# Loading, turning and splitting the left halves of x's first four tiles ahead of the right halves in a two-layer transformer kernel

## The reference

```
q = split_heads(hidden_states @ Wq)      # hidden_states: (2, 1024, 512), Wq: (512, 2048)
k = split_heads(hidden_states @ Wk)
v = split_heads(hidden_states @ Wv)
scores = einsum('bhsd,bhtd->bhst', q, k) * scaling + mask
attn = softmax(scores); out = einsum('bhst,bhtd->bhsd', attn, v)
x = layernorm(x + out @ Wo)
# ... then rows chosen by a router, attention and MLP over them, and a second layernorm
```

## Time and profile before

| | |
|---|---|
| time, median of three executions | 1269.94 us (1269.14 to 1270.07) |
| the profiled execution: time | 1268.86 us |
| the profiled execution: span of the trace | 1267.1 us |
| PE busy | 1252.8 us, 99% |
| DVE busy | 807.0 us, 64% |
| ACT busy | 623.2 us, 49% |
| POOL busy | 245.1 us, 19% |

### The profile page before, as it was taken

One profiled execution on the slowest core, in us unless ns is written; L12 is line 12 of the kernel. 1 busy time (PEld: TensorE's weight loads), 2 busy tenths in 40 slices (PEclk: granted clock), 3 DMA queues, 4 the chain that ended last, 5 costly groups with the idle time before them and its releaser, 6 DMA issues.

```text
span 1267.1 us, 19392 instructions
## 1 busy us (share of the span) xinstructions
PE 1252.8 (99%) x7474; PEld 1103.3 (87%) x7474; DVE 807.0 (64%) x2227; ACT 623.2 (49%) x1448; POOL 245.1 (19%) x216
## 2 busy tenths in 40 slices
PE   9999999999999999999999999999999999999997
PEld 8898989898989898988989898989898987568896
DVE  5555665656555655667776776565656579969633
ACT  5544444444544454555554444445444444558653
POOL 2101111020202020024220211111111113310155
PEclk9999999999999999999999999999999999999999
DMA  6000101010101110203320110110010106565563
GB/s 207 28 25 25 43 17 51 17 51 17 50 18 50 34 51 1 84 18 117 109 96 30 34 34 30 60 34 34 18 51 17 51 18 235 167 216 168 182 217 117
DMA packets 62445, 89.36 MB, mean 71 GB/s; under 512 B 3264, under 2 KB 36032, under 8 KB 62352
## 3 DMA queue, kind: packets, MB, share of 16 engines
q1 hardware_dynamic: 61936, 86.82, 20.8%
q0 software_dynamic: 416, 1.31, 0.3%
HBM read 79.20 MB, written 8.91 MB: 70 GB/s over the span
## 4 chain that ended last, share of the span: by engine, by line
PE 94%; DVE 3%; DMA 1%; ACT 1%; POOL 1%; issue 0%; POOLq 0%
PE proj L1170 45%; PE y L1170 14%; PE s L1170 12%; PE o L1170 10%; PE tp L1263 6%; PE proj L1178 2%; DVE arena L1696 1%; PE s L1178 1%; ACT arena L1480 1%; PE o L1178 1%; DMA late<-rope,position 0%; DMA wraw<-in_L_ffn_wq 0%; PE tp L1399 0%; PE y L1377 0%; DMA yacc<-in_L_attn_hidden_states 0%
## 5 line engine op out<-in xcount | busy, mean ns | idle before, releaser
L1170 PE MATMUL proj<-arena 128*128 128x256 f32 (+1 forms) x3504 | 647.3, 333 | 0.1
L1170 PEld LDWEIGHTS proj<-arena 128*128 128x128 f32 x3504 | 535.5, 189 | 60.2 <-DVE arena L1696 1.1
L2045 POOL TENSOR_TENSOR arena<-wraw,arena 128x1024 fp32r<-128x1024 f32 x73 | 174.8, 2402 | 826.8 <-ACT arena L1480 826.7
L1518 ACT ACTIVATE prob<-prob,stat 128x384 f32<-128x384 f32 (+1 forms) x256 | 150.8, 589 | 363.5 <-DVE stat L1731 363.0
L1696 DVE TENSOR_TENSOR arena<-proj,arena 128x512 fp32r<-128x512 f32 (+1 forms) x256 | 142.2, 557 | 239.7 <-ACT arena L1480 237.0
L1170 PE MATMUL y<-arena 128*128 128x512 f32 x816 | 211.6, 394 | 0.0
L1170 PE MATMUL s<-arena 128*128 128x384 f32 (+2 forms) x912 | 203.6, 338 | 0.7 <-DVE arena L1696 0.6
L1696 DVE TENSOR_TENSOR arena<-tp,arena 128x384 fp32r<-128x384 f32 (+2 forms) x258 | 134.8, 522 | 93.2 <-ACT arena L1480 92.4
L1170 PE MATMUL o<-arena 128*128 128x256 f32 (+2 forms) x966 | 191.9, 319 | 0.0
L1480 ACT ACTIVATE arena<-proj 128x512 fp32r<-128x512 f32 (+1 forms) x256 | 124.3, 486 | 130.7 <-PE proj L1170 114.0
L1170 PEld LDWEIGHTS s<-arena 128*128 128x128 f32 x912 | 157.6, 188 | 17.2 <-DVE arena L1696 1.8
(11 more groups left out here) (163 smaller groups left out, 669.4 us busy)
## 6 DMA issues: line engine op xcount, KB each, us to landing
wraw<-in_L_attn_Wv SPq DMA_DIRECT2D x16, 512.0 KB, 3.4
wraw<-in_L_attn_Wo SPq DMA_DIRECT2D x16, 512.0 KB, 3.7
wraw<-in_L_attn_Wq SPq DMA_DIRECT2D x15, 512.0 KB, 3.4
wraw<-in_L_attn_Wk SPq DMA_DIRECT2D x15, 512.0 KB, 3.4
yacc<-in_L_attn_hidden_states SPq DMA_DIRECT2D x16, 256.0 KB, 3.6
y_dram<-yacc SPq DMA_DIRECT2D x16, 256.0 KB, 2.2
out<-works SPq DMA_DIRECT2D x16, 256.0 KB, 2.7
wraw<-in_L_ffn_wq SPq DMA_DIRECT2D x8, 512.0 KB, 4.6
```

The lines of the kernel that those rows point to most:

```text
L1170: ins = e.matmul(out_ap, l[a], r[b], start=first and i == 0 and j == 0, stop=final and i == n - 1 and j == 2, skip_group_check=skip)
L1518: e.activation(prob[s][:, 0:n], prob[s][:, 0:n], ACT.Exp, bias=stat[:, 4 * s + 1:4 * s + 2], scale=-1.0, accum_out=stat[:, 4 * s + 2:4 * s ...
L2045: e.tensor_tensor(lo, wraw[n % RAW_SLOTS][:], hi.bitcast(F32), ALU.subtract).then_inc(*G_.inc("wsplit", n, "lo"))
```

## The change

The loads, turns and splits of x's tiles 0 to 3 in the first batch are each done in two halves of 256 columns. A new job `residleft` loads the left half of a tile and a new job `turnleft` turns it (two transposes) and makes its high and low part; the old jobs `resid` and `turn` do the right half for these tiles. The right halves are loaded between the two halves of weight piece 0. In the sequence of jobs, `turnleft` stands where `turn` stood; then comes the split of the first half of piece 0 and `qkfirst`; then the four right `turn` jobs, the split of the second half of piece 0, and `qk`; the splits of piece 1 come behind that.

```
+HALVED = 4
...
                     for half in range(2):
                         first_loaded[2 * n + half].plan(n)
                         job("wloadhalf", n, half)
+                        if (n, half) == (0, 0):
+                            for t in range(HALVED):
+                                load_resid(0, t)
...
-        for t in range(4):
-            load_resid(0, t)
+        for t in range(HALVED):
+            left_loaded[t].plan()
+            job("residleft", t)
         load_next(2)
...
         for t, to in enumerate(("tp", "s0", "s1", "o0")):
-            turn_x(0, t, to)
+            hold(to, ("turnleft", t), V_, "turn", 0, t, "lo")
+            job("turnleft", t)
+            bank_of["turn", 0, t] = to
             if t % 2 == 1:
                 job("warm", 1 + t // 2)
-        need("q", 0, 0)
+        job("wfirst", 0, 0)
+        bank_of["qk", 0, "q", 0] = "proj0"
+        hold("proj0", ("qk", 0, "q", 0), V_, "qk", 0, "q", 0, "lo")
+        job("qkfirst", 0, "q", 0)
+        for t in range(HALVED):
+            job("turn", 0, t)
+        job("wfirst", 0, 1)
+        split_on[0], split_to[0] = "V", 1
+        load_next()
+        job("qk", 0, "q", 0)
         need("k", 0, 0)
-        put(project_qk(0, "q", 0))
...
+                elif kind == "turnleft":
+                    t, = key
+                    dst = bank[bank_of["turn", 0, t]]
+                    pe.wait_ge(*freed(bank_of["turn", 0, t], "turnleft", t))
+                    pe.wait_ge(*left_loaded[t].at())
+                    for k in range(KT // 2):
+                        ins = e.transpose(dst[:, k * P:(k + 1) * P], yacc[:, t, k * P:(k + 1) * P], ident[:])
+                    ins.then_inc(*T_.inc("turnleft", t, "made"))
...
-                        pe.wait_ge(*V_.at("turn", b, c * 4 + 3, "lo"))
+                        pe.wait_ge(*(V_.at("turnleft", HALVED - 1, "lo") if (b, c) == (0, 0) else V_.at("turn", b, c * 4 + 3, "lo")))
...
                     else:
                         pe.wait_ge(*split(which, b, h // HG))
+                        pe.wait_ge(*V_.at("turn", b, c * 4 + 3, "lo"))
                         ins = three_passes(e, bank[to][:, :], pairs[KT // 2:], False, True)
```

More of the change, by code:

```diff
@@ L434, in build @@
         resid_loaded = [Landings(semaphore(f"resid_loaded{t}")) for t in range(TT)]
+        left_loaded = [Landings(semaphore(f"left_loaded{t}")) for t in range(HALVED)]
         y_stored = [Landings(semaphore(f"y_stored{t}")) for t in range(TT)]
@@ L448, in build @@
             const=dict(V=("ones", "zeros", "masks", "small"), G=("ident0", "ident", "filled", "small")),
+            turnleft=dict(T=("made",), S=("hi",), V=("lo",)),
             turn=dict(T=("made",), S=("hi",), V=("lo",)),
@@ L1196, in tensor_program @@
                     dst = bank[bank_of["turn", b, t]]
-                    pe.wait_ge(*freed(bank_of["turn", b, t], "turn", b, t))
+                    halved = b == 0 and t < HALVED
+                    if not halved:
+                        pe.wait_ge(*freed(bank_of["turn", b, t], "turn", b, t))
                     if b == 0:
@@ L1204, in tensor_program @@
                         pe.wait_ge(*x_loaded[t % 6].at(b, t))
-                    for k in range(KT):
+                    for k in range(KT // 2 if halved else 0, KT):
                         ins = e.transpose(dst[:, k * P:(k + 1) * P], src[:, k * P:(k + 1) * P], ident[:])
@@ L1492, in scalar_program @@
                         act.wait_ge(*T_.at("qk", NH - 1, "k" if t < 4 else "q", t // 4, "made"))
+                    ks = slice(KT // 2 if b == 0 and t < HALVED else 0, KT)
                     src = bank[bank_of["turn", b, t]][:, :].rearrange("p (k n) -> p k n", k=KT)
                     act.wait_ge(*T_.at("turn", b, t, "made"))
-                    hi_part(xT[0][:, :, t * P:(t + 1) * P], src, "turn", b, t)
+                    hi_part(xT[0][:, ks, t * P:(t + 1) * P], src[:, ks, :], "turn", b, t)
+                elif kind == "turnleft":
+                    t, = key
+                    src = bank[bank_of["turn", 0, t]][:, 0:D // 2].rearrange("p (k n) -> p k n", k=KT // 2)
+                    act.wait_ge(*T_.at("turnleft", t, "made"))
+                    hi_part(xT[0][:, 0:KT // 2, t * P:(t + 1) * P], src, "turnleft", t)
                 elif kind == "qk":
@@ L1709, in vector_program @@
                     cols = slice(t * P, (t + 1) * P)
+                    ks = slice(KT // 2 if b == 0 and t < HALVED else 0, KT)
                     src = bank[bank_of["turn", b, t]][:, :].rearrange("p (k n) -> p k n", k=KT)
-                    lo_part(xT[1][:, :, cols], src, xT[0][:, :, cols], "turn", b, t)
+                    lo_part(xT[1][:, ks, cols], src[:, ks, :], xT[0][:, ks, cols], "turn", b, t)
+                elif kind == "turnleft":
+                    t, = key
+                    cols = slice(t * P, (t + 1) * P)
+                    src = bank[bank_of["turn", 0, t]][:, 0:D // 2].rearrange("p (k n) -> p k n", k=KT // 2)
+                    lo_part(xT[1][:, 0:KT // 2, cols], src, xT[0][:, 0:KT // 2, cols], "turnleft", t)
                 elif kind == "qk":
@@ L2137, in sync_program @@
                                 ).then_inc(first_loaded[2 * n + half].sem, 16)
+                elif kind == "residleft":
+                    t, = key
+                    e.dma_start(yacc[:, t, 0:D // 2], x[0, t * P:(t + 1) * P, 0:D // 2]).then_inc(left_loaded[t].sem, 16)
                 elif kind == "resid":
                     b, t = key
+                    at = D // 2 if b == 0 and t < HALVED else 0
                     if b > 0:
@@ L2144, in sync_program @@
                         sp.wait_ge(*V_.at("lnscore", b - 1, t, "score"))
-                    e.dma_start(yacc[:, t, :], x[b, t * P:(t + 1) * P, :]).then_inc(resid_loaded[t].sem, 16)
+                    e.dma_start(yacc[:, t, at:D], x[b, t * P:(t + 1) * P, at:D]).then_inc(resid_loaded[t].sem, 16)
                 elif kind == "lnorm":
```

## The result

The changed kernel takes 1272.91 us (median of 8 executions, 1271.11 to 1274.12) against 1269.41 (8, 1268.49 to 1270.07): ratio 1.0025, 95% interval 1.0016 to 1.0035, so 2.0 to 4.4 us slower. A second measurement, on the chip of the later experiments, gave 1272.95 (11 executions) against 1270.29 (33): ratio 1.0021 [1.0012, 1.0030]. The forecast was 1272.0 in a range of 1269.5 to 1274.6. The time is in the range and the sign is right. But both points lie a little beyond the 0.2% (2.5 us) that the forecast took as what a measurement can tell from no change, and neither interval takes in 1. So the kernel is slower by a little, and to "slower" the forecast gave 0.39, to "same" 0.57.

The account below looks back on a forecast made before the run. PE was taken as one long queue from 20 us on, so v's start decides: -1.67 + 0.83 + 2.10 + 0.51 + 0.19 + 0.22 - 0.11 = +2.07, median 1272.0 us, range 1269.5 to 1274.6.

Parts of the forecast that it names:

- slower: Verdict that the whole changed kernel is measurably slower, beyond 0.2% (2.5 us); chance 0.39.
- same: Verdict that the whole kernel's time can't be told from no change, within 0.2% (2.5 us); chance 0.57.
- rival B: PE's hole before q's second six takes the clock back to 1.2 GHz, losing about 2; total +4.1, 1274.0; chance 0.13.
- Rival C: x's left halves don't land sooner; q's first six start at 9.25; total +3.4, 1273.3; chance 0.10.
- case A: The forecast itself, for the whole kernel: +2.1 us, own range +1.4 to +2.9; chance 0.62.
- Part 1: Start of q's first six matmuls: at 7.95, when the fillers end, instead of 9.62; -1.67 us.
- Part 2: Right turns on PE: eight transposes behind q's first six, formerly under the filler time; +0.83 us.
- Part 3: PE's hole before q's second six: the second weight half's low part stands behind four right halves on ACT and DVE; +2.10 us.
- Part 4: Work pushed behind the hole: PE waits for piece 1's splits, tile 7's low part and POOL's low part; +0.51, +0.19, +0.22 us.
- The clock: PE's 2.1 us hole at 10.2: no clock loss priced, since 1.44 us of idle time had left the pace high.
- Rival D: Not slower: the 2.1 us vanish in PE's two waits at the end of layer two; 1269.9; chance 0.15 with a neighbouring case.

Follow-up runs that it names:

- e2: Changed kernel with the split of piece 0's second half moved ahead of the four right turns; 1271.86 us, ratio 1.0011 [1.0002, 1.0020] to the old kernel.
- e10: Changed kernel run again without an edit, a single profiled execution; 1271.93 us, mean granted clock 0.998.
- e1: Changed kernel with 34 more filler matmuls between the right turns and q's second six matmuls; 1271.14 us, ratio 1.0008 [0.9999, 1.0017] to the old kernel.
- e4: Changed kernel with both halves of piece 1 split ahead of the copy of q's bank; median 1272.76 us, ratio 1.0019 [1.0010, 1.0028] to the old kernel.
- e0: Changed kernel run again without an edit, on the chip of the other experiments; 1272.95 us (11 executions), ratio 1.0021 [1.0012, 1.0030] to the old kernel.
- e5: Old kernel with one filler matmul instead of 36 ahead of q's projection, leaving PE idle there; 1271.74 us, ratio 1.0012 [1.0003, 1.0021].

## Why the prediction was right, and where it was off

The sign and the schedule of PE, ACT and DVE were right, and the clock was not. That the median fell into the stated range owes something to luck: the range took in rivals B and C, while the forecast's own case A (+1.4 to +2.9) holds the second median (+2.7) and not the first (+3.5), and both stand for executions with a dropped clock, for which A had no term.

**Part 1, the start of the first six (-1.67).** Right in its mechanism: the loads came sooner, tile 3's left half was turned without a wait, and DVE's chain was done at 7.70, as forecast 7.8. What ends last is the fillers, as it said. But it took the clock's rise where the old trace had it. That rise isn't in the granted clock, which reads 1.00 there, but in the fillers' pace: the 36 took 2.17 to 2.84, and the six started at 7.13 to 8.48 in four profiles. The term is -1.14 to -2.49. It was not a constant, because the fillers had ceased to be slack. Rival C is out.

**Part 2 (+0.83).** The eight transposes took from 9.96 to 12.88 - 1.89 = 10.99, that is 1.03 with the tail of the last, against 0.83 without it.

**Part 3, the hole (+2.10).** 1.88 or 1.89 in each of the four profiles by the trace's count, which begins behind that tail, so 2.1 by the forecast's; the distance of the sixes is 4.40 where the forecast had 4.36. The four copies of 256 columns took 10.38 to 11.45, 0.27 each, where 0.28 was taken. e2 shows what the hole hangs on.

**Part 4 (+0.51, +0.19, +0.22).** With the clock kept (e10; e1 has 8.82), the second six are 8.83 from v against 8.76 forecast, and undoing the order of piece 1 (e4) gave back 0.82 of the 0.92.

**The clock.** This is the step that was mis-weighed: rival B, with a chance of 0.13, happened, by the mean clock, in about four executions of five. The earlier trace rows showed that 1.44 us of idle time didn't cost the clock, and e2's 1.36 agrees; 1.89 and 1.95 did (e0, e5), though not always (e4, e10). The Trainium skill ("TensorE: Matmul & The Clock Gate", Part 1) has the rule, named and set aside in the forecast, that a PE left idle goes back to the half clock. These traces agree with it in direction only: the length of idle time that the page asks for is longer than this hole, and the hole was enough in most executions; here the measurement decides. Rival B's price was mis-sized as well: the drop costs 9.69 - 8.83 = 0.86 us at v, not 2, because the waits of part 4 are under its cover. PE is slow just where it would have waited: without these waits v stands 8.01 behind the second six (e4), and 9.69 - 8.01 = 1.68 is half of the 3.4 us at the half level. Beside the drop stands the late start of the first six, up to 1.35 us, in the same executions. So the medians of the two groups are 1.6 us apart in the changed kernel, and 3.2 us in e4, where the drop has no waits to cover. That the late rise and the drop go together was seen in five profiles with the hole of 1.89 (two early and kept, three late and dropped). That the start of the fall hangs on the moment of the rise is not shown, and why a hole of 1.89 us costs the clock in some executions and not in others stays open.

**The sum.** Forecast +2.07 at v. Measured at v: +1.36 with the clock kept early, +2.97, +3.20 and +3.57 with it dropped. The medians' +3.5 and +2.7 fit the second kind. Rival D didn't happen: PE's two waits of layer two are still 2.5 us. The forecast, and these sums, take the rest of the span behind v as fixed. It isn't quite: from v to the end the two profiles of the old kernel have 1248.1 us, the four of the changed one 1249.6 to 1251.0, whether its clock was kept (e10, 1249.8) or not. The experiments, whose work behind v is the same, have 1247.2 (e1) to 1250.2 (e2). So a part of 1.5 to 2.9 us that no term holds stands in the single profiles of the changed kernel; e1 with 1247.2 says that it doesn't come with the change's order and loads each time, and the medians leave no room for it as a fixed cost, since v's shifts already make them up (the two profiled executions of the old kernel, 1268.86 and 1268.98, lie under its medians). A small share of the change in it isn't excluded.

## What to carry to other kernels

Splitting a load so that the first product starts sooner pays only if the second product's operands are ready when the first ends: count the chain of evictions behind the second half before counting the earlier start, and look whose work is pushed behind it. Filler matmuls that hold the clock up are slack only as long as something else ends later. Where the real work would be ready before they end, their own pace, which differs between executions, becomes its start. And a hole that is new to a program needs a measurement of its own, since the nearest row of the old trace was shorter than the length that mattered.

## What the runs showed of the hardware

Idle TensorE for 1.44 us left the clock up (with 1.36 us in e2 11 executions of 11 kept a mean of 0.998 or more). With 1.89 us in the changed kernel 15 of 19, and with 1.95 us in e5 11 of 11, had 0.997 or less. In e4, whose profile has the same 1.89 us, 6 of 11 had 0.997 or less. Fillers in a hole of the same place kept the clock in 11 of 11 (e1). So here a wait of about 1.4 us cost nothing, and one half a microsecond longer mostly did.

Where the clock fell, it fell 1.2, 0.5 and 0.8 us behind the end of the hole in the changed kernel (14.0, 12.8 and 13.3, with PE back at work since 12.88, 12.28 and 12.51), and inside the hole in e5 (9.4, with PE idle from 8.25 to 10.20).

The clock's first rise came at a different moment in each execution, although PE's work up to there was the same: the six fillers at 4.33 took 0.54, 0.68 or 0.85 us (e10, e4, e0). The granted clock reads 1.00 from the start in every profile; the rise shows only in the pace.

More and smaller loads made the later ones late, at the same bytes: tile 4, behind the same 2 MB, was issued at 6.56 and landed 6.0 later in the changed kernel, at 12.6; before it was issued at 4.65 and landed 6.1 later, at 10.8. The whole lateness is that of its issue: SP's queue took 0.48 us for each load ahead of it, and there are 12 of them instead of 8. Nothing waited for tile 4 in either kernel.
